# A layer's two halves copied by ScalarE and added by an accumulating transfer instead of a VectorE sum, in a three-layer CIN kernel

## What is computed

```python
hidden = x
for i in range(3):
    z = jnp.einsum('bmd,bnd->bmnd', x, hidden).reshape(B, -1, D)
    cur = jnp.einsum('bcd,co->bod', z, Ws[i]) + bs[i][None, :, None]
    cur = jax.nn.relu(cur)
    if i != 2:
        hidden, direct = cur[:, :100, :], cur[:, 100:, :]
    else:
        direct = cur
    finals.append(direct)
return jnp.sum(jnp.concatenate(finals, axis=1), axis=-1)   # [512, 400]
```

## Time and profile before

| | us |
|---|---|
| median of 3 executions | 2689.59 (2689.41 to 2690.53) |
| the profiled execution, whole | 2688.37 |
| its span, first to last instruction | 2686.6 |
| PE busy | 2653.5 (99%) |
| DVE busy | 2632.0 (98%) |
| ACT busy | 1781.9 (66%) |
| POOL busy | 121.4 (5%) |

### The profile page before, as it was taken

One profiled execution on the slowest core, in us unless ns is written; L12 is line 12 of the kernel. 1 busy time (PEld: TensorE's weight loads), 2 busy tenths in 40 slices (PEclk: granted clock), 3 DMA queues, 4 the chain that ended last, 5 costly groups with the idle time before them and its releaser, 6 DMA issues.

```text
span 2686.6 us, 53050 instructions
## 1 busy us (share of the span) xinstructions
PE 2653.5 (99%) x17992; PEld 2639.8 (98%) x17992; DVE 2632.0 (98%) x2592; ACT 1781.9 (66%) x2979; POOL 121.4 (5%) x148
## 2 busy tenths in 40 slices
PE   6999999999999999999999999999999999999999
PEld 4999999999999999999999999999999999999998
DVE  6999999999999999999999999999999999999998
ACT  4666666666666666666666666666666666666665
POOL 0000000000000000000000000000000000000000
PEclk8999999999999999999999999999999999999999
DMA  8555545544565455455556544554555455445543
GB/s 197 138 141 140 135 120 134 141 126 122 143 152 135 125 143 132 120 133 139 129 136 152 141 121 125 142 133 120 134 143 129 122 141 139 120 129 142 129 120 72
DMA packets 249093, 358.44 MB, mean 133 GB/s; under 512 B 30584, under 2 KB 183972, under 8 KB 248900
## 3 DMA queue, kind: packets, MB, share of 16 engines
q1 hardware_dynamic: 230038, 331.46, 47.1%
q0 software_dynamic: 18960, 25.76, 5.6%
HBM read 326.67 MB, written 6.60 MB: 124 GB/s over the span
## 4 chain that ended last, share of the span: by engine, by line
PE 98%; DVE 1%; issue 1%; ACT 0%; DMA 0%; SPq 0%; DVEq 0%; ACTq 0%
PE acc L901 64%; PE acc L902 30%; PE acc L894 2%; PE turned L914 1%; PE x_turned L936 1%; DVE z_low L539 0%; DVE z L533 0%; ACT w_split L764 0%; PE x_turned L923 0%; DMA mixed<-in_r_x_dram 0%; DVE z L507 0%; DVE w_split L489 0%; ACT mixed L760 0%; ACT z_high L716 0%; DVE s L549 0%
## 5 line engine op out<-in xcount | busy, mean ns | idle before, releaser
L901 PE MATMUL acc<-w_split,z_high 128*128 128x400 f32 (+1 forms) x8704 | 2603.0, 367 | 21.1 <-DVE z_low L539 17.1
L902 PE MATMUL acc<-w_split,z_low 128*128 128x200 f32 (+1 forms) x8704 | 2221.8, 255 | 0.0
L716 ACT ACTIVATE z_high<-z 128x1024 fp32r<-128x1024 f32 (+2 forms) x1152 | 1165.4, 1012 | 800.7 <-PE acc L902 497.4
L902 PEld LDWEIGHTS acc<-w_split,z_low 128*128 128x128 f32 (+1 forms) x8704 | 1664.8, 191 | 0.0
L901 PEld LDWEIGHTS acc<-w_split,z_high 128*128 128x128 f32 (+1 forms) x8704 | 1637.5, 188 | 24.3 <-issue 17.0
L539 DVE TENSOR_TENSOR z_low<-z,z_high 128x1024 fp32r<-128x1024 f32 (+2 forms) x1152 | 1332.6, 1157 | 20.6 <-ACT z_high L716 8.2
L533 DVE TENSOR_TENSOR z<-mixed,xb 128x1024 f32<-128x1024 f32 (+1 forms) x1024 | 1209.6, 1181 | 1.3 <-DMA xb<-x_by_unit 1.1
L441 POOL DMA_DIRECT2D direct<-fresh_direct x129 | 113.4, 879 | 2327.6 <-ACT fresh_direct L755 2306.7
L741 ACT ACTIVATE mixed<-turned 32x128 f32<-32x128 f32 x768 | 204.9, 267 | 8.9
L738 ACT ACTIVATE mixed<-turned 96x512 f32<-96x512 f32 x256 | 150.6, 588 | 6.0 <-PE turned L914 1.9
L507 DVE TENSOR_TENSOR z<-x_left,x_right 118x896 f32<-118x896 f32 x128 | 138.0, 1078 | 0.0
(11 more groups left out here) (30 smaller groups left out, 97.9 us busy)
## 6 DMA issues: line engine op xcount, KB each, us to landing
xb<-x_by_unit SPq DMA_DIRECT2D x378, 384.0 KB, 5.0
x_right<-x_by_unit SPq DMA_DIRECT2D x384, 136.5 KB
xb<-x_by_unit SPq DMA_DIRECT2D x384, 128.0 KB, 5.7
xb<-x_by_unit SPq DMA_DIRECT2D x126, 336.0 KB
direct<-fresh_direct POOLq DMA_DIRECT2D x115, 200.0 KB, 6.9
xb<-x_by_unit SPq DMA_DIRECT2D x128, 84.0 KB
x_left<-x_by_unit SPq DMA_DIRECT2D x384, 19.5 KB
mixed<-in_L_rec_W_dram SPq DMA_DIRECT2D x5, 600.0 KB, 5.9
```

Of the source, the lines that this page charges most:

```text
L716: nc.scalar.activation(z_high[slot % RING][0:rows, 0:n * T], z[0:rows, slot % RING, 0:n * T], ACT.Copy).then_inc(high, 1)
L901: nc.tensor.matmul(a[:, 0:2 * O], z_high[slot % RING][0:rows, tok], w, start=(c == 0), stop=False, skip_group_check=True)
L902: last = nc.tensor.matmul(a[:, 0:O], z_low[slot % LOW_RING][0:rows, tok], w[:, 0:O], start=False, stop=(c == chunks - 1), skip_group_check ...
```

## The change

Four edits, made together.

1. There is no whole chunk any more: all 31 chunks of layer 2 take the way of the others. Its first group has 8 chunks again for ACT and DVE, and PE has one more pair of matmuls in place of the full-precision one.
2. Layer 2's halves: ACT copies both halves out of `acc`, the first into `s` and the second into `half2` (`halves2`). POOL issues an accumulating transfer from `half2` onto `s` (`sum2`). DVE's `sums2` is gone but for the last unit. PE's layer 2 waits for `half2_in`, ACT's copies, and no longer for the sum.
3. ReLU works in place on `s`. `fresh_direct` is gone: POOL's transfers to `direct` read `s` itself, of which each partition holds four pieces of 100 numbers that don't adjoin.
4. So `s` may be overwritten only when that transfer has landed. `sums` waits for `direct_in` of the same period's transfer in place of `relu_in`; `halves2` waits for the transfer of the period before.

```diff
-WHOLE = 1
...
-        z_both = sb("z", [P, WHOLE * T + RING * GROUP * T])
-        z_whole = z_both[:, 0:WHOLE * T]
-        z = z_both[:, WHOLE * T:].rearrange("p (r e) -> p r e", r=RING)
+        z_all = sb("z", [P, RING * GROUP * T])
+        z = z_all.rearrange("p (r e) -> p r e", r=RING)
...
-        fresh_direct = sb("fresh_direct", [P, 4, HID])
...
             def add(a, b):
-                return pool.dma_start(direct[:, a:b, :].rearrange("p l o -> p (l o)"), fresh_direct[:, a:b, :].rearrange("p l o -> p (l o)"),
+                return pool.dma_start(direct[:, a:b, :], s[:, a:b, 1, 0:HID],
                                       accum_op=ALU.add)
...
-                pool.dma_start(direct[:, a:b, :].rearrange("p l o -> p (l o)"), fresh_direct[:, a:b, :].rearrange("p l o -> p (l o)"))\
+                pool.dma_start(direct[:, a:b, :], s[:, a:b, 1, 0:HID])\
                     .then_inc(direct_new, 16)
 
+            def sum2(u):
+
+                pool.wait_ge(half2_in, u + 1)
+                pool.dma_start(s[:, 2:4, 1, 0:HID], half2, accum_op=ALU.add).then_inc(s2_in, 16)
+
             def period(r, d, n):
+                sum2(n - 2)
 
                 pool.wait_ge(relu_in, n - 1)
...
                 elif added is not None:
-                    dve.wait_ge(relu_in, added - 3)
+
+                    dve.wait_ge(direct_in, 16 * (added - 3))
                 nc.vector.tensor_tensor(s[:, a:b, :, 0:HID], acc[:, a:b, 0:O].rearrange("p l (h o) -> p l h o", o=HID),
                                         half[:, a:b, :, :], ALU.add).then_inc(s_in, 1)
-
-            def sums2(u):
-                dve.wait_ge(half2_in, u + 1)
...
-                lows(base + q, slot(q), P, split_chunks(2, 0))
+                lows(base + q, slot(q), P, group_chunks(0))
...
-            def second_half2(last):
+            def halves2(u, last):
+
                 act.wait_ge(freed, RING + last + 1)
+                if not (isinstance(u, int) and u == 0):
+                    act.wait_ge(direct_in, 16 * u)
+                nc.scalar.activation(s[:, 2:4, 1, 0:HID], acc[:, 2, 0:O].rearrange("p (h o) -> p h o", o=HID), ACT.Copy)
                 nc.scalar.activation(half2, acc[:, 2, O:2 * O].rearrange("p (h o) -> p h o", o=HID), ACT.Copy)\
                   .then_inc(half2_in, 1)
...
-                act.wait_ge(s2_in, n - 1)
+                act.wait_ge(s2_in, 16 * n - 16)
...
-                nc.scalar.activation(fresh_direct[:, a:4, :], s[:, a:4, 1, 0:HID], ACT.Relu).then_inc(relu_in, 1)
+                nc.scalar.activation(s[:, a:4, 1, 0:HID], s[:, a:4, 1, 0:HID], ACT.Relu).then_inc(relu_in, 1)
...
-                if split_from(layer, g):
-                    pe.wait_ge(product, number + 1)
-                    for c in range(WHOLE):
-                        used = nc.tensor.matmul(a[:, 0:O], z_whole[:, c * T:(c + 1) * T], w_whole[:, c, :], start=(c == 0), stop=False,
-                                                skip_group_check=True)
...
-                pe.wait_ge(s2_in, n - 1)
+                pe.wait_ge(half2_in, n - 1)
```

More of the change, by code:

```diff
@@ L72, in group_chunks @@
     return min(GROUP, CHUNKS - GROUP * g)
[L75 to L80, removed]
 def first(n):
@@ L194, in cin_kernel @@
         relu_in = sem("relu_in")
+        sum_last = sem("sum_last")
         direct_in, direct_new, direct_begun = sem("direct_in"), sem("direct_new"), sem("direct_begun")
@@ L242, in piece @@
         def piece(l, g):
-            at = GROUP * g + split_from(l, g) - (WHOLE if l == 2 else 0)
-            return w_split[l][:, at:at + split_chunks(l, g), :]
+            return w_split[l][:, GROUP * g:GROUP * g + group_chunks(g), :]
         def load_w(queue, l, g, w, bias):
             k = GROUPS * (l - 1) + g
-            skip, n = split_from(l, g), split_chunks(l, g)
-            a = GROUP * g + skip
+            n, a = group_chunks(g), GROUP * g
             wt, row = w.tensor, HID * O
             st = stage(l, g)
-            if skip:
-                queue.dma_start(w_whole[0:MAIN, :, :], bass.AP(wt, 0, [[O, MAIN], [row, skip], [1, O]])).then_inc(w_whole_in, 16)
-                queue.dma_start(w_whole[MAIN:P, :, :], bass.AP(wt, CHUNKS * row, [[O, P - MAIN], [row, skip], [1, O]])).then_inc(w_whole_in, 16)
             queue.dma_start(st[0:MAIN, :, :], bass.AP(wt, a * row, [[O, MAIN], [row, n], [1, O]])).then_inc(w_in[k], 16)
@@ L257, in load_w @@
                 queue.dma_start(st[MAIN:P, :, :],
-                                bass.AP(wt, (CHUNKS + skip) * row + 32 * g * O, [[O, P - MAIN], [row, n], [1, O]])).then_inc(w_in[k], 16)
+                                bass.AP(wt, CHUNKS * row + 32 * g * O, [[O, P - MAIN], [row, n], [1, O]])).then_inc(w_in[k], 16)
             else:
@@ L482, in _ @@
                 period(n // D, n % D, n)
+            sum2(UNITS - 2)
         @block.vector
@@ L633, in _ @@
             fresh(1, 2).then_inc(direct_begun, 1)
-            lows(at + 5, at + 5, P, split_chunks(2, 0))
+            lows(at + 5, at + 5, P, group_chunks(0))
             product12(2, 0, 0, 2, at + 7, at + 7)
@@ L658, in period @@
                 lows(base + 2, slot(2), P, group_chunks(2))
-                sums2(n - 2)
                 q = 4
@@ L695, in _ @@
             product12(2, UNITS - 1, 1, 0, at, at)
-            sums2(UNITS - 2)
             for g in range(1, GROUPS):
                 product12(2, UNITS - 1, 1, g, at + g, at + g)
-                lows(at + g - 1, at + g - 1, P, split_chunks(2, g - 1))
+                lows(at + g - 1, at + g - 1, P, group_chunks(g - 1))
             lows(at + 3, at + 3, P, group_chunks(3))
             dve.wait_ge(s_in, ended(UNITS - 1))
-            dve.wait_ge(s2_in, UNITS - 1)
+            dve.wait_ge(s2_in, 16 * (UNITS - 1))
             dve.wait_ge(direct_in, 16 * (UNITS - 2))
@@ L705, in _ @@
             dve.wait_ge(direct_begun, 4)
-            sums2(UNITS - 1)
-            dve.wait_ge(s2_in, UNITS)
+            dve.wait_ge(half2_in, UNITS)
+            nc.vector.tensor_tensor(s[:, 2:4, 1, 0:HID], acc[:, 2, 0:O].rearrange("p (h o) -> p h o", o=HID), half2, ALU.add)\
+              .then_inc(sum_last, 1)
+            dve.wait_ge(sum_last, 1)
             add(2, 4).then_inc(direct_begun, 1)
@@ L818, in _ @@
             hidden(0, 2, 0, ended(0))
-            highs(at + 5, at + 5, P, split_chunks(2, 0))
+            highs(at + 5, at + 5, P, group_chunks(0))
             highs(at + 6, at + 6, P, group_chunks(1))
@@ L848, in period @@
                 relu_direct(r, d, n)
-                highs(base + q, slot(q), P, split_chunks(2, 0))
+                highs(base + q, slot(q), P, group_chunks(0))
                 if turn:
@@ L877, in _ @@
             hidden(1, UNITS - 1, 1, ended(UNITS - 1))
-            second_half2(at - 1)
+            halves2(UNITS - 2, at - 1)
             for g in range(GROUPS):
-                highs(at + g, at + g, P, split_chunks(2, g))
-            act.wait_ge(s2_in, UNITS - 1)
-            second_half2(at + 3)
+                highs(at + g, at + g, P, group_chunks(g))
+            act.wait_ge(s2_in, 16 * (UNITS - 1))
+            act.wait_ge(freed, RING + at + 4)
+            nc.scalar.activation(half2, acc[:, 2, O:2 * O].rearrange("p (h o) -> p h o", o=HID), ACT.Copy).then_inc(half2_in, 1)
         @block.tensor
@@ L887, in multiply @@
             def multiply(layer, number, slot, g=0):
-                c0, n = (0, L0_CHUNKS) if layer == 0 else (GROUP * g + split_from(layer, g), split_chunks(layer, g))
+                c0, n = (0, L0_CHUNKS) if layer == 0 else (GROUP * g, group_chunks(g))
                 rows, chunks = (L0_ROWS, L0_CHUNKS) if layer == 0 else (P, CHUNKS)
                 a = acc[:, layer, :]
-                if split_from(layer, g):
-                    pe.wait_ge(product, number + 1)
-                    for c in range(WHOLE):
-                        used = nc.tensor.matmul(a[:, 0:O], z_whole[:, c * T:(c + 1) * T], w_whole[:, c, :], start=(c == 0), stop=False,
-                                                skip_group_check=True)
-                    used.then_inc(whole_used, 1)
                 pe.wait_ge(low, number + 1)
@@ L899, in multiply @@
                     tok = slice((c - c0) * T, (c - c0 + 1) * T)
-                    w = w_split[layer][0:rows, c - (WHOLE if layer == 2 else 0), :]
+                    w = w_split[layer][0:rows, c, :]
                     nc.tensor.matmul(a[:, 0:2 * O], z_high[slot % RING][0:rows, tok], w, start=(c == 0), stop=False, skip_group_check=True)
@@ L1003, in _ @@
             at = first(UNITS)
-            pe.wait_ge(s2_in, UNITS - 1)
+            pe.wait_ge(half2_in, UNITS - 1)
             for g in range(GROUPS):
```

11 lines of the change are left out of this document (3 added, 8 removed).

## The result

The changed kernel takes 2949.63 us (median of 6, 2936.41 to 2955.33), the kernel before 2689.24 us beside it. The ratio is 1.0959, 95% interval 1.0942 to 1.0976: slower by almost 10%, as forecast in sign and by mechanism; the forecast of 3052 us was 102 us too much. The profiled execution took 2954.21 us with a span of 2952.4.

What follows compares the result with a forecast made beforehand. PE bound the kernel before; the new loop of 14.1 + L (9.2) makes 23.3 us a period, 2.8 more over 126 periods: 2688.4 + 354 + 8 = 3050.4, median 1.2 above, so 3052 us; range 2740 to 3330.

Steps and rivals of the forecast that it cites:

- L: Time from issue to landing of the transfer to `direct`: 9.2 us, bounds 6.9 to 12.
- The bound and the new wait: PE bounds before, DVE 0.23 us behind; afterwards `sums` waiting for the landing closes a loop of 23.3 us a period.
- The links up to the ReLU: From `sums` through layer 0's product on DVE and ACT's `highs` to the ReLU: 13.18 us.
- the base of 6.9: Landing time of the transfer to `direct` before the change, 128 rows of 1600 B: 6.9 us, median of 115.
- the slope of 2.7 ns a packet: POOL's issue: 0.87 against 0.57 us put down to 112 more packets, so 384 more packets add 1.0 us.
- The doubling of this 0.7 to 1.3: Smaller pieces add 0.7 us of DMA engine time; POOL's queue gets about half the full engines, so 1.3 us.
- The ten periods with more transfers: Periods at the tiles' borders issue one or two transfers more ahead of the counted one: some 8 us in all.
- The other new transfer: `half2` onto `s`, due before the ReLU: estimated 4.2 us to land, 5.2 us available, nothing added in the sum.
- the first transfer late too: Rival: the halves' transfer lands at 14.9, delaying the ReLU; 1.7 us more a period, 3266 us; chance 0.10.
- it falls each time: Rival: PE's idle 2.9 us drops TensorE's clock every period, ACT's `highs` waits some 1 us: 3178 us; chance 0.10.
- The transfer lands in time: Rival: L under 6.3 us, so PE bounds at 20.44 us a period: 2684 us; chance 0.08.
- The moved work: Per period PE saves 0.04 to 0.05 us, DVE's work falls 0.14, ACT's additions fit its idle time; 5.7 us gain alone.

Runs made afterwards that it cites:

- long runs: The changed kernel with the ReLU writing its own buffer, so the transfer to `direct` is 128 runs of 1600 B; `sums` still waits for its landing: 2768.02 us.
- the run with the fillers: The changed kernel with five more matmuls per period on PE, results unused, ahead of layer 2's last group: 2933.48 us, ratio 1.0899.
- the split alone: The kernel before with all 31 chunks of layer 2 split and DVE keeping its sum of layer 2's halves: 2697.90 us, ratio 1.0032.

## Why the prediction was right, and what in it was not

The mechanism was right and so was its size to within 102 us of 363 forecast. Part of that closeness is luck: L was over by 1.2 us a period, and a delay of the ReLU by the clock, for which the sum had nothing, made up for 0.4 of it.

- **The bound and the new wait.** Right: DVE idle before `sums` released by the transfer, PE idle behind it, no engine at its limit. Taking the wait out gives all back (2686.65), putting it alone into the kernel before costs 135 us. The waits were forecast as about 3 us a period and are 1.9 for DVE and 1.8 for PE; PE's busy share was forecast as 87% and is 93%, in part for the shorter period, in part because at half the clock a matmul counts for twice as long (12 in place of 24 in 3.3 us).
- **The links up to the ReLU.** 13.18 forecast; 13.26 in the periods without a clock fall, 13.63 over all. The forecast that ACT's `highs` would be released by DVE and no longer by PE held in the periods without a fall.
- **The term that was mis-sized is L**, 9.2 forecast, 8.02 measured; 1.2 us in 126 periods are 150 us too many, against which the later ReLU and issue (0.45 + 0.09) were 68 us too few. Of its three parts: the base of 6.9 was met (6.95 with long runs). The issue was put at 1.0 more than 0.87 and is 1.29, 0.4 more: the slope of 2.7 ns a packet, taken from an accumulating and a plain transfer, did not hold. The rest, 1.3 forecast, is 1.07 - 0.4 = 0.7. The queue's own work was sized well: in the window of 1324.5 to 1329.5 of the changed kernel (the row below) it is 37.5% of 5.0 us, 1.88 us of each engine as forecast, 0.7 more than before. The doubling of this 0.7 to 1.3, for the loads that share the engines, is what was too much. So the two terms put on top of the 6.9 were 2.3 us and measured 1.07, less than half.

```profile
q0 software_dynamic: 528, 0.20, 37.5%
```

- **The ten periods with more transfers** were put at 8 us on top; in the changed kernel they cost nothing: the 9 of them among the 123 average 22.54 us, the others 22.63. With one run per row they are longer, 22.00 against 21.09.
- **The other new transfer.** 4.2 us estimated (its named parts, 0.94, 2 and 1, add up to 3.9), 3.1 measured, where 5.2 were there; "the first transfer late too" did not happen.
- **The clock.** I gave "it falls each time" 0.10, at 1 us a period. It falls in about a quarter of the periods, after a wait of 1.9 us too, and delays the ReLU by 1.35 us there. What that costs on average is 0.13 us a period by the run with the fillers.
- **"The transfer lands in time"** came true in the experiments, not in the change: with an issue 1.7 to 2.1 us sooner. (Its chance was given as 0.08 and then split into 0.05 and 0.04.) The point from which it decides, L under 6.3 at the given place, agrees with one run's 6.95 costing 79 us.
- **The moved work.** PE's gain was forecast as 0.045 us a period and is 0.027 (20.514 to 20.487 between the kernel before and the one without the wait), 2.9 us in all against 5.7. DVE's 0.23 us were called the room it has behind PE; as the split alone shows, only 0.08 of them gave way, and 0.15 stayed as a wait for ACT while DVE's work grew by 0.13. In the change this stayed without effect, since DVE lost its sum of 0.27 us.

The Trainium skill's formula for a transfer from GpSimd (DMA: Bandwidth & Descriptors, section "Anatomy of one DMA — SWDGE (gpsimd) path") would give, as an estimate, 2.2 us for 100 KB. The halves' transfer, in a stretch in which the DMA engines do nothing else, took 3.1; those of 200 KB beside the loads had medians of 4.4 to 8.2.

## What to carry to other kernels

A buffer saved by working in place turns a wait for an engine into a wait for a transfer's landing. Follow that wait round: if what it holds back leads to the next such transfer, the period is the sum of the links, landing included, and no engine's busy share shows it. Then look for the link that can be shortened for nothing: here one instruction moved ahead of five on ACT was worth 256 us. And a small regular wait of an engine close to the bound isn't slack until it is known what it waits for.

## What I had not expected of the hardware

- The time to landing of one and the same transfer differs with its place before or among the loads: 6.95 or 4.77 us for 128 runs of 1600 B, 8.02 or 6.88 for 512 of 400 B, the shorter ones with the ReLU 1.7 and 2.1 us sooner in the period and the issue ahead of the first load of `xb`.
- POOL's time to issue an accumulating transfer grew with its pieces, but not in proportion: 0.87 to 0.91 us for 128, 1.19 for 256 (the halves' transfer, from another source to another destination), 1.29 for 512.
- TensorE's granted clock fell to half (1.2 GHz) after a wait of 1.9 us, but not after one of 2.57 us in the same trace. In the opening of the kernel before, it had fallen after a wait of 3.20 us, and I took that as the nearest row.
